# A two-layer graph network on one core: the order of SyncE's loads and stores in layer one

## What is computed

```python
def _rel_layer(h, src, dst, etype, norm, V, comp, loop_w, bias, activation):
    c = comp[etype]                       # 8 coefficients for each edge
    for b in range(8):
        m = m + c[:, b, None] * (h @ V[b])[src]
    agg = segment_sum(m * norm, dst)
    out = agg + bias + h @ loop_w         # relu in the first layer
def _gcn_conv(x, W, b, src, dst, norm):
    return segment_sum((x @ W)[src] * norm, dst) + b
```

## Time and profile before

| what | value |
|---|---|
| median of 3 runs | 2055.03 us (2051.82 to 2055.29) |
| the profiled execution, its own time | 2051.85 us |
| its span, first to last instruction | 2050.1 us |
| busy: PE, DVE, POOL, ACT | 83%, 68%, 68%, 17% of the span |
| mean granted TensorE clock | 0.894 |
| layer one, layer two, dense stages | about 50 to 1011 us, 1011 to 1903 us, 1903 us to the end |

### The profile page before, as it was taken

One profiled execution on the slowest core, in us unless ns is written; L12 is line 12 of the kernel. 1 busy time (PEld: TensorE's weight loads), 2 busy tenths in 40 slices (PEclk: granted clock), 3 DMA queues, 4 the chain that ended last, 5 costly groups with the idle time before them and its releaser, 6 DMA issues. The chain is left out here.

```text
span 2050.1 us, 40639 instructions
## 1 busy us (share of the span) xinstructions
PE 1695.4 (83%) x12305; PEld 1222.6 (60%) x12306; DVE 1398.6 (68%) x2294; ACT 356.9 (17%) x869; POOL 1401.6 (68%) x1527
## 2 busy tenths in 40 slices
PE   1488888888888888888579888889999899968998
PEld 1366656556656656566457666666666666755564
DVE  7887887787887887787677666666566657511443
ACT  2032222222222222222101011010110111101300
POOL 5777777777777777777277777777777777777000
PEclk8589889989889899989789899999999999968999
DMA  5334334434334334333222222233233332334463
GB/s 147 92 95 113 99 95 106 98 89 110 98 88 111 98 89 111 96 95 90 57 58 64 57 61 60 57 83 101 80 89 84 82 97 77 91 93 127 146 231 121
DMA packets 194039, 196.66 MB, mean 96 GB/s; under 512 B 109132, under 2 KB 157273, under 8 KB 193946
## 3 DMA queue, kind: packets, MB, share of 16 engines
q0 software_dynamic: 45760, 93.81, 18.3%
q1 hardware_dynamic: 140134, 97.59, 16.6%
q10 hardware_dynamic: 8052, 4.04, 0.7%
HBM read 169.75 MB, written 25.57 MB: 95 GB/s over the span
## 5 line engine op out<-in xcount | busy, mean ns | idle before, releaser
L811 POOL DMA_INDIRECT ring<-h_rows,rel_idx x1312 | 1255.9, 957 | 401.1 <-issue 370.4
L982 DVE TENSOR_TENSOR rel_pick<-rel_src_row,dve_bank 128x1664 bf16<-128x1664 int32 (+1 forms) x268 | 485.7, 1813 | 184.4 <-PE rel_ps_p L1211 85.6
L1280 PE MATMUL rel_ps_z<-rel_C,ring 128*128 128x56 f32 x3100 | 418.7, 284 | 192.0 <-DVE ring L988 101.9
L1280 PEld LDWEIGHTS rel_ps_z<-rel_C,ring 128*128 128x128 f32 x3100 | 401.2, 201 | 242.6 <-issue 232.2
L1378 ACT ACTIVATE rel_ZT<-rel_ps_z 128x304 f32 x292 | 114.2, 426 | 1109.3 <-PE rel_ps_z L1280 1107.7
L1224 PE MATMUL rel_ps_p<-rel_h_parts,rel_pick 128*128 128x384 bf16 x1150 | 266.6, 362 | 0.0
L1368 ACT ACTIVATE rel_A<-rel_ps_a 128x500 f32 x292 | 165.5, 603 | 368.0 <-PE rel_ps_a L1168 212.4
L1211 PE MATMUL rel_ps_p<-rel_h_parts,rel_pick 128*128 128x384 bf16 x1100 | 196.6, 338 | 22.0 <-DVE rel_h_parts L970 22.0
L1211 PE MATMUL carried<-rel_h_parts,rel_pick 128*128 128x384 bf16 x1100 | 194.9, 336 | 2.4 <-DVE rel_pick L982 2.4
L1168 PE MATMUL rel_ps_a<-rel_M,rel_lo 128*128 128x175 bf16 x784 | 154.7, 302 | 24.9 <-DVE rel_M L949 24.9
L1211 PEld LDWEIGHTS rel_ps_p<-rel_h_parts,rel_pick 128*128 128x128 bf16 x1100 | 111.3, 103 | 96.5 <-issue 33.7
(11 more groups left out here) (232 smaller groups left out, 1711.8 us busy)
## 6 DMA issues: line engine op xcount, KB each, us to landing
ring<-h_rows,rel_idx POOLq DMA_INDIRECT x1312
A_slabs<-rel_A SPq DMA_DIRECT2D x25, 800.0 KB
A_slot<-A_slabs SPq DMA_DIRECT2D x25, 800.0 KB, 4.5
rel_types<-edge_types SPq DMA_DIRECT2D x97, 200.0 KB
early_slot<-A_slabs SPq DMA_DIRECT2D x18, 896.0 KB, 6.0
rel_src_row<-in_src_dram SPq DMA_DIRECT2D x134, 64.0 KB, 3.2
last_slot<-A_slabs SPq DMA_DIRECT2D x4, 512.0 KB, 5.9
ring<-h_rows,idx_table POOLq DMA_INDIRECT x118
```

Of the source, the lines that this page charges most:

```text
L811: g_.indirect_dma_start(ring[:, s * CHUNK + i, :], None, rows_in, bass.IndirectOffsetOnAxis(ap=idx[which][:, n:n + 1], axis=0)).then_inc(l ...
L982: v.tensor_tensor(pick[:, b0:b0 + n, :], src_row[s][:, :].unsqueeze(1).to_broadcast(shape), node_ids[:, b0:b0 + n].unsqueeze(2).to_broadca ...
L1280: ins = m_.matmul(bank(ps_z[s], NB)[:, :, bass.ds(at[i], TW)], ring[:, first + i, :], C[s][:, i, :, :], start=False, stop=(i == n - 1))
```

## The change

In layer one only, SP's order within a group is another. In every chunk the type load comes first. The source-row loads that were made at j == 1 and j == 3 are made one chunk later, at j == 2 and at j == 0 of the next group. The store of the slab moves from j == 1 to j == 3, behind the type loads of chunks 2 and 3; in the last group, which has two chunks, it moves from j == 1 to j == 0. No DMA is added or dropped, and no wait of a DMA is changed.

```diff
                     for j in range(chunks_of(g)):
                         if makes(g, j):
                             co.load(sp, g * CPG + (j + AHEAD), (j + AHEAD) % 4)
-                        if j % 2 == 1 and not (isinstance(g, int) and not first_picks((g + 1) * CPG + j)):
-                            load_sources(g, j)
-                        if j == 1 and not is_group(g, 0):
+                        if j % 2 == 0 and not is_group(g, 0):
+                            behind = (g, 1) if j == 2 else (g - 1, 3)
+                            if not (isinstance(g, int) and not first_picks((behind[0] + 1) * CPG + behind[1])):
+                                load_sources(*behind)
+                        if is_group(g, 0) and j == 2:
+                            load_sources(0, 1)
+                        if j == (0 if is_group(g, GROUPS - 1) else 3) and not is_group(g, 0):
                             sp.wait_ge(a_kept, (g * CPG + 1) * 2)
                             store_slab(g - 1, 1 - parity)
```

## The result

The changed kernel takes **2035.70 us** in the median of 6 runs (2035.23 to 2040.13), the kernel before 2053.54 in 6 runs (2046.90 to 2055.29). The ratio is **0.9927 [0.9916, 0.9938]**, faster by 0.7%; the two medians alone lie a little further apart, 17.8 us or 0.9%. The profiled execution took 2035.34 us with a span of 2033.6, against 2051.85 and 2050.1.

What follows compares the result with a forecast made beforehand. Two chains at one pace: POOL's full gathers, and the later DVE-PE loop ending layer one. Of 81 us waits removed, 41 reach PE and 16.4 the end: 2051.85 - 16.4 = 2035.5, as a median 2038.5; range 2027 to 2050.

Steps and rivals of the forecast that it cites:

- The types' wait goes entirely: DVE's waits for edge-type tables, 81.0 us in 25 waits, vanish once type loads go ahead of the store.
- What the loop gets, 1.86 us a group and 41 offered: Loop of DVE and PE: DVE's picked row comes 1.86 us earlier each group, 41 us over 22 groups.
- wait for wait: Rival, chance 0.10: DVE begins earlier but waits for PE as long, PE ends last; no difference, 2055 us.
- Used this up in some 14 groups: Layer one: the loop, 25.3 us behind POOL, closes in within 14 groups; then PE waits for gathers.
- What the end gets, 16.4 us at chunk 96: End of layer one: z of chunk 96 starts at 970.1 instead of 986.5, limited by its last gather's landing.
- Gathers' lengthening, taken as 0 within 9: POOL's gathers beside DVE's one-hots: always hit costs 5 to 9 us, never hit gains as much; taken as 0.
- POOL slowed: Rival, chance 0.06: gathers starting during DVE's one-hots lengthen; slower, 2062 us at a mean of 1.00.
- The clock at the end, 3 us either way and taken as 0: PE's chunk 96 at granted clock 0.53: 3 us less at full clock, or as much more; taken as 0.
- Source rows moved: 0: SP's 46 source-row loads, used two to three chunks later, go out when they do today; cost 0.
- The store: same time, at least 7.3 us of cover for the fold: Store at j == 3 leaves as today or at most an issue later; DVE's fold keeps at least 7.3 us.
- The order is not the cause: Rival, chance 0.06: DMA engines' load, not queue place, makes tables late; DVE's waits stay, 2055 us.
- POOL not full: Rival, chance 0.03: POOL does not bind, so all 41 us of the loop's gain arrive; 2014 us.

Runs made afterwards that it cites:

- e9: Kernel before with only the store moved to j == 3, ahead of the source row there; source rows stay at j == 1 and j == 3: 2036.76 us, ratio 0.9925.
- e12: Kernel before with SP's order kept, but the store issued by ACT on its own queue: 2035.41 us, ratio 0.9912.
- e5: Changed kernel with 45 gathers of layer one left out (eighth tile of even chunks from chunk 8 on): 2028.96 us, ratio 0.9884.
- e10: Kernel before with only the source-row loads moved one chunk later, the store staying at j == 1: 2055.09 us, ratio 1.0007.
- e11: Kernel before with the store moved to j == 3 but behind the source row there: 2170.17 us, ratio 1.0557.
- e6: Changed kernel with the fold's four slab additions left out, the last addition staying: 2027.79 us, ratio 0.9871.

## Why the prediction was right, point by point

- **The number.** 2038.5 against 2035.70; against the profiled executions, 16.4 us forecast and 16.5 found (2051.85 - 2035.34). That they agree so closely is luck: only 14.0 of the 16.5 lie in layer one, and the loop's gain was taken twice too large, as the next points show.
- **The types' wait goes entirely**: right. e9 and e12 show the cause: the queue place.
- **What the loop gets, 1.86 us a group and 41 offered**: mis-sized by two. It was 0.97. Two steps failed. The 1.86 us by which the row comes earlier were the reading of a single group, in which PE stood 2.01 us; the mean wait at j = 1 was 1.48, and the row came 1.28 earlier. And "from there to the next group I find nothing on the way that gives it back" overlooked that the clock drop can move: PE's stretch behind M now runs at 0.68 instead of 0.88, DVE's degree waits for its end, and 0.42 a group is given back. That the slab follows PE was wrong too: the slab of j = 3 waits for DVE's M in both kernels, 10.1 us behind the row. It did not hurt since, as the prediction said, 0.75 a group was enough. That was a margin of 0.2 us a group, not of 1.1: the rival wait for wait was nearer than its 0.10.
- **"Used this up in some 14 groups"**: wrong with it. PE reached POOL at chunks 92 to 94. e5 puts the gain that POOL cuts off at 6.7 us.
- **What the end gets, 16.4 us at chunk 96**: 14.5, for POOL came to that gather's end 1.9 us later (970.3 against 968.4). "POOL's gathers still ending near 976" (977.8) and "about 19" for the gap (20.3) are off by the same 1 to 2 us.
- **Gathers' lengthening, taken as 0 within 9**: the mean rose from 968 to 972 ns, 2.5 us over 613. The place was half read. I priced the one-hots alone, and by the overlaps the excess beside them did grow, by 1.6 us; but the fold weighs more beside fewer us of DVE (7.0 us beside 41, against 5.1 beside 65) and grew by 1.3, while L948 lost 1.1 (before, as L944, 3.3). The rival POOL slowed needed 0.022 and got 0.004. Its 92 one-hot pairs are 87 by its own numbers (23.6 / 0.27); nothing rests on that.
- **The clock at the end, 3 us either way and taken as 0**: right. z of chunk 96 takes 3.63 us as before. e5, with no wait before it, shows the other level: 1.96.
- **Source rows moved: 0**: right (e10). But their move is what lets the store leave in time (e11), which the prediction did not say.
- **The store: same time, at least 7.3 us of cover for the fold**: right. It leaves at 525.27 in a group whose fold starts at 539.91, 14.6 us later, unwaited. e11 shows the price once the cover is gone.
- **The order is not the cause**: excluded by e9 and e12. **POOL not full**: excluded by PE's wait at 971.99 and by e5.

## What to carry to other kernels

When a transfer that is released late is moved on a queue, look at what it then stands behind and what stands behind it: by the medians, the same store in the same chunk gained 18 us ahead of the source row and lost 117 behind it. Take a loop's gain from its period over many rounds, since one group is not the mean, a later product of another engine sets its own pace, and the clock takes its part, and count it for the end only as far as the next full chain lies away.

## What the runs showed of the hardware

- **The fold's float16 additions on DVE, with both operands in SBUF, lengthen gathers that GpSimd issues at the same time**: without them the mean went from 972 to 958 ns and POOL ended the layer 8.6 us earlier (e6). The Trainium skill (SBUF — State Buffer, Who interferes with whom) says that such an addition contends with GpSimd's reads, and infers that it leaves descriptor writing alone. By that inference the gathers would have kept their length; here they did not. What in the additions does it is not shown. M, the pick and C take both operands from SBUF as well, and beside their 106, 117 and 41 us of overlap the gathers' excess is 0.4, 0.3 and 0.1 us. A gather also reads its row numbers (`rel_idx`) from SBUF, so it may be that read which is held up.
- **The clock drop goes where the wait goes.** The slow stretch (0.78 before at j = 2, 0.75 after at j = 3) follows PE's wait of 2.01 or 1.51 us. Over twenty groups the clock of j = 2 went from 0.86 to 1.00 when the wait before it fell from 1.48 to 0.20 us. What a drop costs depends on whether a wait stands behind it.
- **A load behind a store of 800 KB is late**: 8.3 us from issue to use in the earlier trace rows, and its own issue took 2.94 to 3.31 us in 22 groups of the kernel before, where the issue of any other table took 0.28 to 0.75 us. The store's own landing releases the fold 5.7 us after its issue (e11).
- **One chip runs this program 24% slower** (2537.63 us), with stops of about 1 us in PE's own issue. What causes them stays open, and the "instruction supply" of an expectation above is a guess; no order of DMAs showed there.
